# An attention and feed-forward block on one core: normalized rows turned by transposing DMAs, down products in their own PSUM bank, context parts split in one run

## The chip, the cores and the metric

The kernel runs on one core of a Trainium2 chip. The metric is the device time of one execution in microseconds, lower being better. The core has five engines with a queue each: PE (TensorE, matmuls), DVE (VectorE), ACT (ScalarE), POOL (GpSimd) and SP (SyncE, which here only issues DMAs). Engines wait for one another by semaphores alone.

## The reference

```python
h = tok_attention(x)                                   # 64 sequences, channels x 512 positions
h = h + attn(layernorm(h), Wq, Wk, Wv, Wo, qn_w, kn_w) # 16 heads, 4 kv heads, rms norm, rope, causal softmax
h = h + ffn(layernorm(h), w1, w2, w3)                  # bitlinear(sigmoid(x1) * x2), w quantized to -1, 0, 1
# ffn: x1 = y @ quant(w1).T ; x2 = y @ quant(w2).T ; out = (sigmoid(x1) * x2) @ quant(w3).T
```

The output has 64 x 32 rows of 512 numbers. The model width is 512, the head width 128, the feed-forward width 1408.

## The kernel before, in words

There are two stages. The first (`token_attention`) computes the token attention, writes its rows to `h1` in DRAM, and meanwhile converts the weights: the attention weights to pairs of float16 (a high and a low part), the feed-forward weights to ternary float16. The change does not touch it. The second (`blocks`) works through the 2048 rows in 16 tiles of 128 rows. Each engine has its own program, written out by hand in `body(n, attn, ffn)` and run over n = 0 to 16 by `over_tiles` (L654): n = 0 does attention alone, n = 1 to 14 is a loop, n = 15 and 16 are the last ones. Pass n works on the attention half of tile n and on the feed-forward half of tile n-1, interleaved.

The layernorm of a tile is computed with rows on partitions. The matmuls need it with features on partitions, in two float16 parts. In the kernel before PE does the turning: `transpose_x` (L1002) and `transpose_x2` (L1007) each issue four 128x128 float32 transposes into a PSUM bank (TR[0] and TR[1]); ACT copies the bank to the high part (`take_x` L729, L769), and DVE subtracts to get the low part (`x_low` L820, L890).

PE's order in a pass (L1098) is: projections c = 1 to 3 (`project`, 12 matmuls each, three products for each pair of parts), the transposes of x2n of tile n-1, projections 4 and 5; the gate products (`gate_products`, L1026 and L1027) of tile n-1 in six groups, with the transposes of rotated k and q (`transpose_qk`, L967 through `transpose`) and the scores (L1044) between them; the first 8 of 11 pairs of down products (L1062, L1063); the transposes of xn of tile n+1; the probabilities times the values (`weigh_values`, L1076); the other 3 pairs of down products; the projection c = 0 (keys) of tile n+1; and 48 output products (L1090 to L1092). Down products and output products accumulate in the same bank, PROJ[1], so the output products wait until DVE has read the down products (L942, semaphore `o_out`).

DVE makes the rotation of each projection (`rotate`, L832 to L847), the softmax chain (L910 to L930), the low context parts (`context_lo`, L867, four for each tile, behind ACT's four high parts L791), the result (L942) and the residual with its layernorm statistics (L953 and `ln_stats`). The result stands between the second and the third context part. POOL adds and scales the rotated projections (`rope_sum`, L700 to L707) and takes inverse square roots (L696). ACT squares, applies tanh and exp, and copies PSUM to SBUF.

Of the kernel before, what the change touches and what calls it, by code (L numbers as in the profile page):

```python
# [16 lines left out]
P = 128  # L17
# [551 lines left out]
def blocks(nc, W, h1, tables_in, norm_in, mask_in, ident_in, out):  # L569

    with ExitStack() as ctx:
# [9 lines left out]
        SCORES = TR[1]  # L581
# [14 lines left out]
        xh, xl = sb("x_hi", [P, D], F16), sb("x_lo", [P, D], F16)  # L596
# [20 lines left out]
        x2h, x2l = sb("x2_hi", [P, D], F16), sb("x2_lo", [P, D], F16)  # L617
# [9 lines left out]
        xt, x_hi, x_lo = sem("b_xt"), sem("b_x_hi"), sem("b_x_lo")  # L627
# [11 lines left out]
        xt2, x2_hi, x2_lo = sem("b_xt2"), sem("b_x2_hi"), sem("b_x2_lo")  # L639
# [10 lines left out]
        BANK = (PROJ[0], FB[2], FB[3], PROJ[0], PROJ[1], TR[0])  # L650
        DOWN_FIRST = 8
# [19 lines left out]
        @block.sync  # L671
        def _(sp):
            sp.dma_start(h_ln[:, :], h1[0:P, :]).then_inc(ln_in, DMA)
            for dst, src in ((tables[:, :, :], tables_in), (norm_w[:, :, :], norm_in), (mask[:, :], mask_in),
                             (ident[:, :], ident_in)):
                sp.dma_start(dst, src).then_inc(const_in, DMA)

            def body(n, attn, ffn):
                if attn and not (isinstance(n, int) and n + 1 >= NTT):
# [5 lines left out]
                if ffn:  # L685
                    sp.wait_ge(o_out, n + START)
                    sp.dma_start(out[bass.ds((n - 1) * P, P), :], o_tile[:, :]).then_inc(out_done, DMA)

            over_tiles(sp, body)
            sp.wait_ge(out_done, DMA * NTT + START)  # L690

        @block.gpsimd
        def _(pool):
# [14 lines left out]

            pool.wait_ge(const_set, 1)
            inv_std(0, 0, ln1_var, ln1_rstd)  # L710
            rope_sum(0, 0)
# [14 lines left out]
        def _(act):  # L726
            def take_x(n):
                act.wait_ge(xt, n + 1)
                nc.scalar.copy(xh[:, :], TR[0][:, :]).then_inc(x_hi, 1)  # L729
# [32 lines left out]
            def body(n, attn, ffn):  # L762
                last = isinstance(n, int) and n + 1 >= NTT
                if attn:
                    for c in range(1, KV):
                        square(n, c)
                if ffn:
                    act.wait_ge(xt2, n)
                    nc.scalar.copy(x2h[:, :], TR[1][:, :]).then_inc(x2_hi, 1)  # L769
                if attn:  # L770
                    square(n, KV)
                    act.wait_ge(proj, NPROJ * (n + 1))
                    nc.scalar.mul(v[:, :], BANK[NPROJ - 1][:, :], V_SHIFT).then_inc(v_out, 1)
                for f in range(NF):
                    for m in range(2):
# [5 lines left out]
                        if attn and (f, m) == (NF - 1, 1):  # L781
                            act.wait_ge(sub, n + 1)
                            nc.scalar.activation(pr[:, :, :], sd[:, :, :], ACT.Exp).then_inc(exped, 1)
                        if ffn and m == 1:
                            hidden_hi(n - 1, f)
                if attn:
                    if not last:
                        take_x(n + 1)
# [9 lines left out]
        def _(dve):  # L798
# [18 lines left out]

            def x_low(n):
                dve.wait_ge(x_hi, n + 1)
                nc.vector.tensor_tensor(xl[:, :], TR[0][:, :], xh[:, :], ALU.subtract).then_inc(x_lo, 1)  # L820
# [55 lines left out]
            x_low(0)  # L876
            rotate(0, 0)

            def body(n, attn, ffn):
# [5 lines left out]
                if attn:  # L885
                    for c in range(2, KV):
                        rotate(n, c)
                if ffn:
                    dve.wait_ge(x2_hi, n)
                    nc.vector.tensor_tensor(x2l[:, :], TR[1][:, :], x2h[:, :], ALU.subtract).then_inc(x2_lo, 1)  # L890
                if attn:
                    rotate(n, KV)
# [20 lines left out]
                if attn:  # L913
# [5 lines left out]
                    if not last:  # L919
                        ln_apply(n + 1, 0, h_ln[:, :], xn[:, :], ln1_rstd, ln1)  # L920
# [13 lines left out]
                if attn:  # L934
                    if not last:
                        x_low(n + 1)
                    for b in range(2):
                        context_lo(n, b)
                if ffn:
                    dve.wait_ge(w3, n)  # L940
                    dve.wait_ge(out_done, DMA * (n - 1) + START)
                    nc.vector.scalar_tensor_tensor(o_tile[:, :], PROJ[1][:, :], 2.0 ** -6, h2[:, :], ALU.mult, ALU.add  # L942
                                                   ).then_inc(o_out, 1)
                if attn:
                    for b in range(2, BT):
                        context_lo(n, b)
# [14 lines left out]
        def _(pe):  # L961
# [16 lines left out]
            def project(n, c):  # L978

                if c == 0:  # L980
                    pe.wait_ge(x_hi, n + 1)
                    pe.wait_ge(x_lo, n + 1)
# [9 lines left out]
                if c == 4 and not first:  # L992
                    pe.wait_ge(h2_done, n)
                pairs = []
                for k in range(KD):
                    at = (K_AT + k * KV * HD if c == 0 else V_AT + k * KV * HD if c == NPROJ - 1
                          else Q_AT + k * HEADS * HD + (c - 1) * D)
                    pairs.append((xh[:, k * P:(k + 1) * P], xl[:, k * P:(k + 1) * P],
                                  W.hi(at, D), W.lo(at, D)))
                split_products(BANK[c][:, :], pairs, proj)  # L1000

            def transpose_x(n):  # L1002
                pe.wait_ge(ln1, n + 1)
                pe.wait_ge(qkt_out, 5 * n)
                transpose(TR[0], xn, xt)

            def transpose_x2(n):  # L1007
                pe.wait_ge(ln2, n + 1)
                pe.wait_ge(taken, n + 1)
                transpose(TR[1], x2n, xt2)  # L1010

            def gate_products(n, f, m):

                if f == 0 and m == 0:
                    pe.wait_ge(x2_hi, n + 1)
                    pe.wait_ge(x2_lo, n + 1)
# [4 lines left out]
                for j, t in enumerate(FG[f]):  # L1021
                    for k in range(KD):
# [3 lines left out]
                        nc.tensor.matmul(dst, w, x2h[:, k * P:(k + 1) * P], start=(k == 0), stop=False)  # L1026
                        ins = nc.tensor.matmul(dst, w, x2l[:, k * P:(k + 1) * P], start=False, stop=(k == KD - 1))  # L1027
                ins.then_inc(f1, 1)

            def transpose_qk(n, c, ffn):  # L1030
                pe.wait_ge(q_ready, 5 * n + c + 1)
                if c == 0:
                    pe.wait_ge(v_out, n + 1)
                if c == 1 and ffn:
                    pe.wait_ge(x2_lo, n)
# [13 lines left out]
            def down_products(n, tiles):  # L1049
                if tiles[0] == 0:  # L1050
                    if isinstance(n, int) and n + 1 >= NTT:
                        pe.wait_ge(h2_done, n + 1)
                    else:
                        pe.wait_ge(squared, 5 * (n + 1) + 5)
                        pe.wait_ge(roped_b, 5 * (n + 1) + 5)
                for k in tiles:
# [5 lines left out]
                    nc.tensor.matmul(PROJ[1][:, :], hh[:, k, :], ffn_w[:, at:at + D], start=(k == 0), stop=False)  # L1062
                    ins = nc.tensor.matmul(PROJ[1][:, :], hl[:, k, :], ffn_w[:, at:at + D], start=False,  # L1063
# [16 lines left out]
            def output_products(n, ffn):  # L1080
                if ffn:
                    pe.wait_ge(o_out, n + START)
# [12 lines left out]
            transpose_x(0)  # L1095
            project(0, 0)

            def body(n, attn, ffn):  # L1098
                last = isinstance(n, int) and n + 1 >= NTT
                if attn:  # L1100
                    for c in range(1, NPROJ - 2):
                        project(n, c)
                if ffn:
                    transpose_x2(n - 1)
                if attn:
                    for c in range(NPROJ - 2, NPROJ):
# [13 lines left out]
                if attn and not last:  # L1120
                    transpose_x(n + 1)
# [4 lines left out]
                if attn:  # L1126
                    if not last:
                        project(n + 1, 0)
                    output_products(n, ffn)
# [61 lines left out]
```

## Time and profile before

| | |
|---|---|
| median of 3 runs | 1173.87 us (1173.56 to 1178.07) |
| profiled execution | 1172.51 us, of it span 1170.6 us |
| PE busy | 1093.5 us, 93% |
| DVE busy | 721.0 us, 62% |
| POOL busy | 433.5 us, 37% |
| ACT busy | 422.2 us, 36% |
| PE in the chain that ended last | 51% |

The first stage and the conversion of the weights end at about 390 us; the block stage takes the rest of the span. A page of the profile gives the busy time of each engine; the timeline lists each instruction with its start and duration, and in square brackets how long the engine had been idle before it and who released it. Matmuls are pipelined: the duration of one in the timeline is longer than the distance from its start to the next one's, and it is the distance that counts.

### The profile page before, as it was taken

What the parts mean: (1) busy time and instruction counts of PE and PEld (TensorE: products, weight loads), DVE (VectorE), ACT (ScalarE), POOL (GpSimd) and SP (SyncE); (2) the same over time, 40 slices, a digit from 0 to 9 for tenths busy, and PEclk for the clock granted to TensorE, in tenths of its full rate; (3) what the DMA queues carried; (4) which work ended last, traced back from release to release, by engine and by line L of the source; (5) the groups of instructions that cost most, each with busy time, mean ns of one, the idle gap of its engine ahead of it and who ended that gap; (6) DMA issues with size and microseconds to landing.
All of it is one profiled execution on the core that took longest, in us unless ns stands there. A gap on an engine that the chain in (4) does not pass through costs nothing.

```text
span 1170.6 us, 22169 instructions
## 1 busy us (share of the span) xinstructions
PE 1093.5 (93%) x8768; PEld 607.9 (52%) x8768; DVE 721.0 (62%) x1293; ACT 422.2 (36%) x733; POOL 433.5 (37%) x334
## 2 busy tenths in 40 slices
PE   4999989899989669999999999999999999999987
PEld 2434333433343235574664665756646657566465
DVE  6687766766685355566556655765666467556642
ACT  1666556455546122232332322313323224123231
POOL 2001027655555246144242361442433514514320
PEclk9999989989989779999999999999999999999999
DMA  6988835643541100000000000000000000000000
GB/s 182 305 312 272 292 116 150 179 132 116 158 133 50 57 10 10 18 9 27 18 9 27 18 9 27 0 27 18 9 27 18 9 27 0 27 18 9 18 11 10
DMA packets 35767, 83.81 MB, mean 72 GB/s; under 512 B 4496, under 2 KB 5264, under 8 KB 35728
## 3 DMA queue, kind: packets, MB, share of 16 engines
q1 hardware_dynamic: 35728, 83.26, 23.0%
q8 instruction: 27, 0.44, 0.2%
q14 instruction: 12, 0.10, 0.0%
HBM read 49.43 MB, written 8.39 MB: 49 GB/s over the span
## 4 chain that ended last, share of the span: by engine, by line
PE 51%; DVE 8%; issue 4%; POOL 2%; ACT 0%; DMA 0%; SPq 0%; DVEq 0%; POOLq 0%
PE ffn_sum L1026 5%; PE ffn_sum L1027 5%; PE proj L1090 5%; PE proj L1091 4%; PE proj L1092 4%; PE proj L973 3%; PE transposed L967 3%; PE proj L974 3%; PE proj L975 3%; PE ffn_sum L975 2%; PE ffn_sum L974 2%; PE ffn_sum L973 2%; PE ffn_sum L1076 2%; PE transposed L1044 1%; PE proj L1062 1%
## 5 line engine op out<-in xcount | busy, mean ns | idle before, releaser
L334 DVE TENSOR_REDUCE row_max<-score_rows 128x1 f32<-128x512 f32 x256 | 167.5, 686 | 90.5 <-PE score_rows L474 89.1
L700 POOL TENSOR_TENSOR roped<-rope_cos,rope_sin 128x512 f32<-128x512 f32 x80 | 101.7, 1271 | 324.8 <-DVE rope_sin L836 324.8
L293 ACT ACTIVATE exps<-score_cols 128x512 f32<-128x512 f32 x256 | 146.3, 600 | 136.4 <-PE score_cols L499 134.4
L1026 PE MATMUL ffn_sum<-x_hi,ffn_w 128*128 128x128 f16 x1408 | 166.9, 220 | 1.4 <-ACT x_hi L769 1.4
L1027 PE MATMUL ffn_sum<-x_lo,ffn_w 128*128 128x128 f16 x1408 | 166.8, 220 | 0.0
L474 PE MATMUL score_rows<-k_parts,q_parts 96*128 96x512 f32 x256 | 127.1, 510 | 16.4 <-DMA k_parts<-qk_low 15.1
L1026 PEld LDWEIGHTS ffn_sum<-x_hi,ffn_w 128*128 128x128 f16 x1408 | 138.1, 98 | 6.4 <-DVE hidden L853 3.0
L1027 PEld LDWEIGHTS ffn_sum<-x_lo,ffn_w 128*128 128x128 f16 x1408 | 138.4, 98 | 2.3
L474 PEld LDWEIGHTS score_rows<-k_parts,q_parts 96*128 96x128 f32 x256 | 53.4, 210 | 131.9 <-DVE row_max L334 73.7
L499 PE MATMUL score_cols<-q_parts,k_parts 98*128 98x512 f32 x256 | 110.0, 435 | 6.7 <-DMA q_parts<-max_t 4.4
L1090 PE MATMUL proj<-attn_slots,ctx_hi 128*128 128x512 f16 x256 | 97.0, 379 | 2.6 <-DVE ctx_lo L867 2.6
L735 ACT ACTIVATE squares<-ffn_sum 128x512 f32<-128x512 f32 x32 | 19.1, 597 | 220.2 <-PE ffn_sum L975 190.4
L1092 PE MATMUL proj<-attn_slots,ctx_lo 128*128 128x512 f16 x256 | 97.0, 379 | 0.0
L1091 PE MATMUL proj<-attn_slots,ctx_hi 128*128 128x512 f16 x256 | 97.0, 379 | 0.0
L248 POOL TENSOR_TENSOR qk_low<-qk_raw,qk_high 128x1024 fp32r<-128x1024 f32 x16 | 38.9, 2433 | 143.7 <-ACT qk_high L287 143.7
L707 POOL TENSOR_TENSOR roped<-roped,rms_inv 128x512 f32<-128x512 f32 x80 | 83.3, 1041 | 11.5
L703 POOL TENSOR_TENSOR rms_inv<-mean_sq,minus_half 128x4 f32<-128x4 f32 x80 | 85.2, 1066 | 3.3
L853 DVE SCALAR_TENSOR_TENSOR hidden<-tanh,ffn_sum 128x512 f32<-128x512 f32 (+1 forms) x48 | 30.8, 641 | 85.8 <-PE ffn_sum L1027 85.8
L953 DVE SCALAR_TENSOR_TENSOR h<-proj,o_unscale,h_res 128x512 f32<-128x512 f32 x16 | 12.0, 751 | 115.9 <-PE proj L1092 115.9
L973 PE MATMUL proj<-attn_slots,x_hi 128*128 128x512 f16 x192 | 74.4, 388 | 1.6 <-DVE x_lo L820 1.6
L974 PE MATMUL proj<-attn_slots,x_hi 128*128 128x512 f16 x192 | 74.3, 387 | 0.0
L975 PE MATMUL proj<-attn_slots,x_lo 128*128 128x512 f16 x192 | 74.2, 386 | 0.0
(124 smaller groups left out, 2010.9 us busy)
## 6 DMA issues: line engine op xcount, KB each, us to landing
raw_ffn<-in_w_ffn SPq DMA_DIRECT2D x24, 704.0 KB, 7.6
attn_slots<-in_w_attn SPq DMA_DIRECT2D x20, 512.0 KB, 11.3
qk_raw<-in_qk SPq DMA_DIRECT2D x16, 512.0 KB, 5.8
q_parts<-qk_high SPq DMA_DIRECT2D x32, 256.0 KB, 3.3
k_parts<-qk_high SPq DMA_DIRECT2D x32, 256.0 KB, 4.2
v_t<-in_v_t SPq DMA_DIRECT2D x16, 256.0 KB, 5.8
q_parts<-qk_low SPq DMA_DIRECT2D x16, 256.0 KB, 4.9
k_parts<-qk_low SPq DMA_DIRECT2D x16, 256.0 KB, 5.2
```

The costliest lines, as they stand in the source:

```text
L293: nc.scalar.activation(E[:, (STEPS * g + u) % NE, :], ST[(STEPS * g + u) % 3][:, :], ACT.Exp, scale=TOK_SCALE).then_inc(exp_done, 1)
L334: nc.vector.reduce_max(row_max[:, g % 2, k:k + 1], S[n % NS][:, :], AX.X).then_inc(s_free, 1)
L474: nc.tensor.matmul(bank[:, :], QP[g % NB][0:3 * CH, b, t * P:(t + 1) * P], KP[g % NB][0:3 * CH, b, :], start=True, stop=True).then_inc(s_f ...
L499: nc.tensor.matmul(ST[n % 3][:, :], KP[g % NB][0:3 * CH + 2, b, i * P:(i + 1) * P], QP[g % NB][0:3 * CH + 2, b, :], start=True, stop=True) ...
L973: nc.tensor.matmul(dst, ah, bh, start=(i == 0), stop=False)
L974: nc.tensor.matmul(dst, ah, bl, start=False, stop=False)
L975: t = nc.tensor.matmul(dst, al, bh, start=False, stop=(i == len(pairs) - 1))
L1026: nc.tensor.matmul(dst, w, x2h[:, k * P:(k + 1) * P], start=(k == 0), stop=False)
L1027: ins = nc.tensor.matmul(dst, w, x2l[:, k * P:(k + 1) * P], start=False, stop=(k == KD - 1))
L1090: nc.tensor.matmul(PROJ[1][:, :], ah, bh, start=(k == 0), stop=False)
L1091: nc.tensor.matmul(PROJ[1][:, :], ah, bl, start=False, stop=False)
L1092: ins = nc.tensor.matmul(PROJ[1][:, :], al, bh, start=False, stop=(k == HEADS - 1))
```

## The change

- The normalized rows are split before they are turned: ACT casts `xn` to `xhr` (float16, rows on partitions), POOL subtracts to get `xlr` for the first layernorm; for the second ACT makes `x2hr` and DVE `x2lr`. SP then issues one transposing DMA for each (`turn_x`, `turn_x2`), SBUF to SBUF, 128x512 float16, into `xh`, `xl`, `x2h`, `x2l` of shape 128 x 4 x 128. PE waits for 32 counts of `x_turned` or `x2_turned` for each tile. SP's program is written out for all 17 passes in place of the loop.
- PE has no transposes of x and x2 any more. The projection c = 0 of tile n+1 stands ahead of `weigh_values`, and the down products are divided into 4 pairs before and 7 pairs behind it.
- The down products accumulate in TR[0] (`DOWN`), the values' projection in TR[1].
- DVE splits all four context parts and then makes the result. The apply step of the next tile's layernorm moves ahead of the second `gate`, and ACT's cast of it behind the last copy of q.

```diff
-        SCORES = TR[1]
+        SCORES, DOWN = TR[1], TR[0]
-        BANK = (PROJ[0], FB[2], FB[3], PROJ[0], PROJ[1], TR[0])
-        DOWN_FIRST = 8
+        BANK = (PROJ[0], FB[2], FB[3], PROJ[0], PROJ[1], TR[1])
+        DOWN_FIRST = 4
@@ SP
+            def turn_x(n):
+                sp.wait_ge(x_hi, n + 1)
+                sp.dma_start(xh[:, :, :], xhr[:, :], transpose=True).then_inc(x_turned, DMA)
+                sp.wait_ge(x_lo, n + 1)
+                sp.dma_start(xl[:, :, :], xlr[:, :], transpose=True).then_inc(x_turned, DMA)
+            turn_x(0)
             def body(n, attn, ffn):
...
                 if ffn:
+                    turn_x2(n - 1)
+                if more:
+                    turn_x(n + 1)
+                if ffn:
                     sp.wait_ge(o_out, n + START)
                     sp.dma_start(out[bass.ds((n - 1) * P, P), :], o_tile[:, :]).then_inc(out_done, DMA)
@@ POOL
+            def x_low(n):
+                pool.wait_ge(x_hi, n + 1)
+                nc.gpsimd.tensor_tensor(xlr[:, :], xn[:, :], xhr[:, :], ALU.subtract).then_inc(x_lo, 1)
...
                     inv_std(n + 1, 0, ln1_var, ln1_rstd)
+                    x_low(n + 1)
                     rope_sum(n + 1, 0)
@@ ACT
             def take_x(n):
-                act.wait_ge(xt, n + 1)
-                nc.scalar.copy(xh[:, :], TR[0][:, :]).then_inc(x_hi, 1)
+                act.wait_ge(ln1, n + 1)
+                nc.scalar.copy(xhr[:, :], xn[:, :]).then_inc(x_hi, 1)
...
                 if attn:
-                    for c in range(1, KV):
+                    square(n, 1)
+                if ffn:
+                    act.wait_ge(ln2, n)
+                    nc.scalar.copy(x2hr[:, :], x2n[:, :]).then_inc(x2_hi, 1)
+                if attn:
+                    for c in range(2, KV + 1):
                         square(n, c)
...
+                        if attn and not last and (f, m) == (1, 0):
+                            take_x(n + 1)
@@ DVE
                     ln_apply(n - 1, 1, h2[:, :], x2n[:, :], ln2_rstd, ln2)
-                if attn:
-                    for c in range(2, KV):
+                if ffn:
+                    dve.wait_ge(x2_hi, n)
+                    nc.vector.tensor_tensor(x2lr[:, :], x2n[:, :], x2hr[:, :], ALU.subtract).then_inc(x2_lo, 1)
+                if attn:
+                    for c in range(2, KV + 1):
                         rotate(n, c)
...
                     hidden_lo(n - 1, 0)
+                if attn and not last:
+                    ln_apply(n + 1, 0, h_ln[:, :], xn[:, :], ln1_rstd, ln1)
+                if ffn:
                     gate(n - 1, 1)
...
-                    if not last:
-                        ln_apply(n + 1, 0, h_ln[:, :], xn[:, :], ln1_rstd, ln1)
...
                 if attn:
-                    if not last:
-                        x_low(n + 1)
-                    for b in range(2):
+                    for b in range(BT):
                         context_lo(n, b)
...
-                    for b in range(2, BT):
-                        context_lo(n, b)
@@ PE
                 if c == 0:
-                    pe.wait_ge(x_hi, n + 1)
-                    pe.wait_ge(x_lo, n + 1)
+                    pe.wait_ge(x_turned, 2 * DMA * (n + 1))
...
                 if tiles[0] == 0:
                     if isinstance(n, int) and n + 1 >= NTT:
-                        pe.wait_ge(h2_done, n + 1)
+                        pe.wait_ge(o_out, n + START)
                     else:
-                        pe.wait_ge(squared, 5 * (n + 1) + 5)
-                        pe.wait_ge(roped_b, 5 * (n + 1) + 5)
+                        pe.wait_ge(qkt_out, 5 * (n + 1) + 5)
...
                 if ffn:
                     down_products(n - 1, range(0, DOWN_FIRST))
                 if attn and not last:
-                    transpose_x(n + 1)
+                    project(n + 1, 0)
                 if attn:
                     weigh_values(n, ffn)
                 if ffn:
                     down_products(n - 1, range(DOWN_FIRST, KF))
                 if attn:
-                    if not last:
-                        project(n + 1, 0)
-                    output_products(n, ffn)
+                    output_products(n)
```

## Rows read from the trace of the kernel before

**Rows 1.** Windows, passes 1 to 14: us; busy (count) PE, PEld, DVE, ACT, POOL; clock, DMA.

```profile
448.84:1099.39 650.55, 644.37 (x5742) 399.13 (x5741) 396.58 (x770) 184.99 (x336) 247.89 (x238) 1.00 0.05 17
```

**Rows 2.** Waits of PE from 440 to 1170 us: total, times, longest.

```profile
PE ffn_sum L1076 <- DVE probs_t L930: 6.2, 14, 0.4
```

**Rows 3.** Timeline of PE, 707 to 741: start, duration, line, operation, operands, [idle before].

```profile
707.72 0.38 PE L1062 MATMUL proj<-ffn_w,hidden_hi 128*128 128x512 f16 x1
...
712.22 0.61 PE L1076 MATMUL ffn_sum<-probs_t,v 32*128 32x128 f32 x12 [0.44 <-DVE probs_t L930]
...
717.30 0.38 PE L1090 MATMUL proj<-attn_slots,ctx_hi 128*128 128x512 f16 x1
...
735.42 0.60 PE L967 MATMUL transposed<-ident,x2n 128*128 128x128 f32 x4
735.86 0.38 PE L973 MATMUL proj<-attn_slots,x_hi 128*128 128x512 f16 x1
...
741.04 0.22 PE L1026 MATMUL ffn_sum<-x_hi,ffn_w 128*128 128x128 f16 x1
```

**Rows 4.** Timeline of DVE in the same pass, 707 to 716.

```profile
707.94 0.69 DVE L917 TENSOR_TENSOR scores_less_max<-scores,row_maxima 128x512 f32<-128x512 f32 x1
...
714.07 1.29 DVE L867 TENSOR_TENSOR ctx_lo<-ffn_sum,ctx_hi 128x512 f16<-128x512 f32 x2 [0.88 <-ACT ctx_hi L791]
715.28 0.68 DVE L942 SCALAR_TENSOR_TENSOR out_tile<-proj,h 128x512 f32<-128x512 f32 x1
```

**Rows 5.** Timeline of DVE and PE in tile 0 and in pass 15.

```profile
435.16 2.48 DVE L867 TENSOR_TENSOR ctx_lo<-ffn_sum,ctx_hi 128x512 f16<-128x512 f32 x4 [2.33 <-ACT ctx_hi L791]
...
1126.14 0.69 DVE L917 TENSOR_TENSOR scores_less_max<-scores,row_maxima 128x512 f32<-128x512 f32 x1
...
1130.14 0.61 PE L1076 MATMUL ffn_sum<-probs_t,v 32*128 32x128 f32 x12 [0.60 <-issue]
```

**Rows 6.** Timeline of DVE, POOL, ACT and PE, 733 to 749.

```profile
733.80 0.53 DVE L815 TENSOR_SCALAR x2n<-h,mv,rstd 128x512 f32<-128x512 f32 x1
...
735.19 0.41 DVE L836 TENSOR_TENSOR rope_sin<-ffn_sum,tables 128x256 f32<-128x256 f32 x1
...
736.36 1.27 POOL L700 TENSOR_TENSOR roped<-rope_cos,rope_sin 128x512 f32<-128x512 f32 x1
...
745.55 1.04 POOL L707 TENSOR_TENSOR roped<-roped,rms_inv 128x512 f32<-128x512 f32 x1
...
747.10 0.64 ACT L747 ACTIVATE hidden_hi<-hidden 128x512 f16<-128x512 f32 x1
...
748.16 0.61 PE L967 MATMUL transposed<-ident,roped 128*128 128x128 f32 x4
...
748.86 0.58 ACT L756 COPY q_t<-transposed 128x512 f32<-128x512 f32 x1
```

**Rows 7.** DMA issues by line: count, KB each, median us to landing; first stage last.

```profile
out<-out_tile SPq DMA_DIRECT2D x16, 256.0 KB, 2.0
...
h_ln<-h_rows SPq DMA_DIRECT2D x13, 256.0 KB, 2.7
...
v_t<-in_v_t SPq DMA_DIRECT2D x13, 256.0 KB, 5.8
```

**Rows 8.** Timeline of DVE and PE at the stage's start and end.

```profile
395.06 0.55 DVE L815 TENSOR_SCALAR xn<-h_ln,mv,rstd 128x512 f32<-128x512 f32 x1
...
398.36 0.58 PE L973 MATMUL proj<-attn_slots,x_hi 128*128 128x512 f16 x1 [1.57 <-DVE x_lo L820]
...
422.82 0.66 PE L967 MATMUL transposed<-ident,roped 128*128 128x128 f32 x4 [2.73 <-POOL roped L707]
...
438.48 0.38 PE L1090 MATMUL proj<-attn_slots,ctx_hi 128*128 128x512 f16 x1
...
1148.52 0.55 DVE L815 TENSOR_SCALAR x2n<-h,mv,rstd 128x512 f32<-128x512 f32 x1 [0.67 <-POOL rstd L696]
...
1151.22 0.26 PE L1026 MATMUL ffn_sum<-x_hi,ffn_w 128*128 128x128 f16 x1 [1.45 <-ACT x_hi L769]
```

More of the change, by code:

```diff
@@ L595, in blocks @@
         xn = sb("xn", [P, D])
-        xh, xl = sb("x_hi", [P, D], F16), sb("x_lo", [P, D], F16)
+        xhr, xlr = sb("x_hi_rows", [P, D], F16), sb("x_lo_rows", [P, D], F16)
+        xh, xl = sb("x_hi", [P, KD, P], F16), sb("x_lo", [P, KD, P], F16)
         sq = [sb(f"squares{n}", [P, D]) for n in range(2)]
@@ L626, in blocks @@
         ln2_var, ln2_rstd, ln2 = sem("b_ln2_var"), sem("b_ln2_rstd"), sem("b_ln2")
-        xt, x_hi, x_lo = sem("b_xt"), sem("b_x_hi"), sem("b_x_lo")
+        x_turned, x_hi, x_lo = sem("b_x_turned"), sem("b_x_hi"), sem("b_x_lo")
         proj, squared, ssum, roped_a, roped_b = (sem("b_proj"), sem("b_squared"), sem("b_ssum"), sem("b_roped_a"),
@@ L676, in _, with turn_x2 @@
                 sp.dma_start(dst, src).then_inc(const_in, DMA)
+            def turn_x(n):
[3 more added lines that the diff above has]
+                sp.dma_start(xl[:, :, :], xlr[:, :], transpose=True).then_inc(x_turned, DMA)
+            def turn_x2(n):
+                sp.wait_ge(x2_hi, n + 1)
+                sp.dma_start(x2h[:, :, :], x2hr[:, :], transpose=True).then_inc(x2_turned, DMA)
+                sp.wait_ge(x2_lo, n + 1)
+                sp.dma_start(x2l[:, :, :], x2lr[:, :], transpose=True).then_inc(x2_turned, DMA)
+            turn_x(0)
             def body(n, attn, ffn):
-                if attn and not (isinstance(n, int) and n + 1 >= NTT):
+                more = attn and not (isinstance(n, int) and n + 1 >= NTT)
+                if more:
                     sp.wait_ge(ln1, n + 1)
@@ L685, in body @@
                 if ffn:
+                    turn_x2(n - 1)
+                if more:
+                    turn_x(n + 1)
+                if ffn:
                     sp.wait_ge(o_out, n + START)
                     sp.dma_start(out[bass.ds((n - 1) * P, P), :], o_tile[:, :]).then_inc(out_done, DMA)
-            over_tiles(sp, body)
+            for n in range(NTT + 1):
+                body(n, n < NTT, n > 0)
             sp.wait_ge(out_done, DMA * NTT + START)
@@ L993, in project @@
                     pe.wait_ge(h2_done, n)
+                if c == NPROJ - 1 and not first:
+                    pe.wait_ge(taken, n)
                 pairs = []
@@ L997, in project @@
                           else Q_AT + k * HEADS * HD + (c - 1) * D)
-                    pairs.append((xh[:, k * P:(k + 1) * P], xl[:, k * P:(k + 1) * P],
-                                  W.hi(at, D), W.lo(at, D)))
+                    pairs.append((xh[:, k, :], xl[:, k, :], W.hi(at, D), W.lo(at, D)))
                 split_products(BANK[c][:, :], pairs, proj)
[L1002 to L1010, printed above, removed]
             def gate_products(n, f, m):
                 if f == 0 and m == 0:
-                    pe.wait_ge(x2_hi, n + 1)
-                    pe.wait_ge(x2_lo, n + 1)
+                    pe.wait_ge(x2_turned, 2 * DMA * (n + 1))
                     pe.wait_ge(c_hi, KV * (n + 1))
@@ L1100, in body @@
                 if attn:
[L1101 to L1106, printed above, removed]
+                    for c in range(1, NPROJ):
                         project(n, c)
```

44 lines of the change are left out of this document (16 added, 28 removed).

## The prediction

> **What bounds the kernel now.** I read four views, in this order. First the windows: the fourteen loop passes that carry the whole change (n = 1 to 14) take 650.55 us, 46.47 us each, with PE busy 644.37 us and the granted clock at 1.00, that is the 2.4 GHz level [rows 1]. PE is the bound there, at full speed, so only what leaves PE's queue, or an idle gap of PE, can shorten a pass. Second the waits of PE: over the stage one gap repeats, 14 times 0.44 us, the product with the probabilities (L1076) waiting for the transposed probabilities from DVE [rows 2]. Third the timeline of PE in the pass that starts at 672 us. 24 projection matmuls stand between 735.86 and 741.04, so one costs 0.216 us; the transposes of x2n occupy PE from 735.42 to 735.86; behind the first down products, which begin at 707.72, and the transposes of xn, L1076 begins only at 712.22 [rows 3]. Fourth DVE and ACT beside it, to see what each wait of the new order would find [rows 4 to 6].
>
> **The change, part by part, in one pass (clock times are those of the pass in the rows).**
>
> *Transposes of x2n leave PE:* 0.44 us (735.42 to 735.86), nothing else was waited for there. Gain 0.44.
>
> *Transposes of xn leave PE, and the project(n+1, 0) block comes before the probability product.* Before, from the first down product (707.72) to L1076 (712.22) are 4.50 us, with 16 down products, the transposes and the gap. After, the same stretch holds 8 down and 12 projection matmuls: 20 x 0.216 = 4.32. Does DVE let L1076 start then? From the subtraction of the row maxima (707.94) to L1076 were 4.28 us. The apply step of xn sat in that stretch of DVE's program (L920), and it now moves ahead of the chain. In the last attention pass, which has no xn step, the same distance is 1126.14 to 1130.14, 4.00 us [rows 4, 5]. PE arrives 707.72 + 4.32 - 707.94 = 4.10 after the subtraction, so the softmax chain (4.00) is just hidden by 0.1 and the 0.44 us gap goes. Gain 4.50 - 4.32 = 0.18.
>
> *From L1076 to the output products.* Before 5.08 us (712.22 to 717.30) [rows 3]: the product, 6 down, 12 projection. DVE split two context parts (714.07), made the result (715.28), and split two more. After, PE holds the product (1.10) and 14 down products (3.02), 4.12; but the output products want all four parts, and these now run without the result between. In tile 0, where nothing was between, four took 2.48 us [rows 4, 5]: 714.07 + 2.48 + 0.15 of release = 716.70, which is 4.48 after L1076's start. So this part is bound by ACT and DVE, with a new stall of 0.36 us on PE. Gain 5.08 - 4.48 = 0.60. Bounds: 0.96 if the parts come in time, 0.00 if ctx_lo still needs what it needed before.
>
> *The result (L942)* waits for the last down product, now at about the time the fourth part ends; it comes 1 us later than before and pushes rotate(n+1, 0) by as much. POOL, its reader, has nothing else between the fifth q part of one pass and that rotation, and DVE then waits for the 48 output products (10.35 us, 48 x 0.216). Transposes of q and k in TR[0] wait for the result, half a pass later. All at nothing. The down products have their own bank, so the output products no longer wait for the result: it was already out of the way, nothing. The result's store and the next h_ln load are issued behind it on SP, 1 us later, while h_ln is not read before the rotations of the next pass: nothing.
>
> *x2 turned by DMAs.* x2n ends at 734.33 (733.80 + 0.53). ACT's cast from SBUF takes 0.64, DVE's subtraction 0.69, as its other steps of this shape [rows 4, 6]: high rows at 735.0, low rows at 735.75. The gate products, first readers, start at 741.04 - 0.44 = 740.60. So the second DMA may take up to **4.85 us** from issue to landing. Behind these waits on SP stand the next x's DMAs and the result's store, which come later anyway. DVE waits for ACT here, and rotate(n, 2) starts 1.44 us later; POOL, busy with the part before, took that part up only at 736.36 where it was ready at 735.60, so the q parts come some 0.7 later. The fifth was ready at 745.55 + 1.04 = 746.59 and its transposes on PE began at 748.16 [rows 6]; with 747.3 against 747.72, 0.4 remains. Cost nothing, 0.4 us of cover; were POOL another us late, a pass would cost 0.6 more.
>
> *x turned by DMAs.* ACT casts x behind the last q copy: 748.86 + 0.58 - 0.44 = 749.0, plus 0.64. The new POOL subtraction is not in the trace; nearest is POOL's addition of the same shape, 1.27 [rows 6] (bounds: 1.04, the multiplication's row, to 2.5, twice the row). Low rows at 751.0. project(n+1, 0) comes at 754.19 (707.72 + 46.47) - 0.44 + 8 x 0.216 = 755.47. So this DMA may take up to **4.4 us**. ACT, while it waits for xn, holds the next hidden_hi, which stands behind two more groups of gate products: nothing.
>
> *What a transposing DMA takes.* No row shows one. Nearest are the plain DMAs of this stage: 256 KB from SBUF in 2.0 us, to SBUF in 2.7 (ours have half the bytes). In the heavy traffic of the first stage a load of 256 KB lands in 5.8 [rows 7]. DMA share here is 0.05 [rows 1]. I take 3.0 for the second of a pair (2.7 and a little for the one ahead of it), with 2.0 and 5.8 as ends. At 3.0 both are hidden.
>
> The Trainium skill speaks on both sides. "VectorE: DVE Perf Modes", The three transpose paths, gives 1309 ns for a 128x128 block by DMA (390 ns by TensorE) and says to use TensorE if a PSUM destination is acceptable. If that price held per block, an estimate from the page is 4 x 1.3 = 5.2 us for each transfer and 10.5 for a pair; the second would land some 9.8 us after its issue, and by my slope below the kernel would be about 155 us slower. "Advanced Engine Details and Errata", X-Bar Transpose, says that transposing DMAs are as fast as regular ones, which would be my 2.0 to 2.7. No row of before decides between them.
>
> *Sum of a pass:* 0.44 + 0.18 + 0.60 = 1.22 us; x 14 = **17.1 us**.
>
> *Edges.* Start: xn ended at 395.61 and the first projection began at 398.36, 2.75 later; after: cast 0.64, POOL 1.27, DMA 3.0, some 5.2: **+2.4**. Tile 0: its last q transposes began at 422.82; in a pass x's low rows come 3.3 after these (751.0 + 0.44 - 748.16), here at 426.1, landed 429.1; twelve projections take 2.6 at the full clock and 5.2 at half, I take 3.9 behind the idle time, 433.0; and 4.48 on is 437.5 against 438.48: **-1.0**. Pass 15: 0.44 + 0.60 = **-1.0**. Last gate products: x2n ends 1149.07, they began 1151.22; after: 0.64 + 0.69 + 3.0 + releases = 1153.4: **+2.2** [rows 5, 8]. Together +2.6.
>
> Net -14.5: span 1170.6 becomes 1156.1, with the 1.9 us around the span 1158.0. That execution (1172.51) was 1.36 below the median of the runs, 1173.87, so **1159.4 us**.
>
> **The rivals.** With t for the second DMA's time from issue to landing, beyond 4.85 each us costs 28 in the passes (two stalls in each of 14) and 4 at the edges, 32 in all; at 4.9 the gain is gone.
> (A) *The turned rows land late*: PE waits before the gate products and before project(n+1, 0). At t = 5.8 (the row of v_t) a pass changes by -1.22 + 0.95 + 1.40 = +1.13, x 14 = 15.8, and the edges by +12 (2.6 and 3 x 2.8, and 1.0 in pass 15): about **1202 us**. For it: nothing measured is a transposing DMA, two are on one queue, PE is full around both. Against: the stage's DMA rows are 2.0 to 2.7 and the cover is 4.4.
> (B) *The context chain keeps PE where it was*: if ACT's casts and DVE's parts need the 5.08 us of before, or POOL's extra work delays the q parts, a pass gains 0.44 + 0.18 only, 8.7 us in all, 2.6 given back: **1168 us**. For it: the end of a pass is bound by this chain in my own sum. Against: tile 0's four parts.
> (C) *PE idles less than the rows say, or the DMAs take 4.6 to 5.1*: gain and stalls cancel, about **1174 us**.
>
> **How the numbers follow.** Forecast 0.50, (A) 0.30, (B) 0.13, (C) 0.07. A difference of 0.5% (5.9 us) is about what a measurement of this kernel can tell from no change. Of (B) half lies within it: faster 0.50 + 0.06, same 0.07 + 0.07, slower 0.30. Lower end: no context stall (-5) and t = 2.0 (-3): 1152. Upper end: (A) at t = 5.8, 1202; beyond lies some 0.17. The forecast's own range is 1152 to 1166.
>
> **What would show it.** Right: passes of about 45.25 us; no PE transposes of x; the transposing DMAs landing below 4.4 us; no PE wait before L1026 and L973; a small one (0.3 to 0.4) before L1090 on ctx_lo; none or under 0.1 before L1076. Wrong: PE waits released by DMA x_hi or x_lo fourteen times (A); waits of L1090 near 1 us or of L967 on POOL's roped (B). A transposing DMA that holds SP's queue for microseconds would also break the sum, since the low rows queue behind the high ones.

## The result and the profile after

The changed kernel takes **1163.37 us** (median of 6 runs, 1161.4 to 1164.11) against 1173.98 us for the kernel before in the same comparison: a ratio of **0.9908, 95% interval 0.9894 to 0.9921**. That is 0.9% faster. I had forecast 1159.4 us, 1.2% faster, in a range of 1152 to 1202 (1152 to 1166 for the forecast's own case). The profiled execution took 1163.83 us, with a span of 1161.7 us, 8.9 less than that of before.

The head of the page of the changed kernel:

```profile
span 1161.7 us, 21798 instructions
## 1 busy us (share of the span) xinstructions
PE 1078.6 (93%) x8640; PEld 592.2 (51%) x8640; DVE 721.7 (62%) x1277; ACT 419.9 (36%) x733; POOL 463.8 (40%) x350
```

PE has lost 15 us of work (1093.5 before). POOL has gained 30 us: 18.6 for its 16 new subtractions (1.16 each), 7.4 because its 32 inverse square roots (L718) take 0.78 us each where they took 0.55, and 3.0 in its multiplications (L729). Why the old steps take longer was not tried. The windows of the changed kernel run from the output products (L1096) of one pass to those of another: the first row is fourteen passes, the second the last thirteen of them. The columns are those of [rows 1].

```profile
440.44:1076.66 636.22, 633.61 (x5629) 385.85 (x5630) 397.73 (x756) 183.09 (x336) 275.29 (x252) 1.00 0.11 28
487.07:1076.66 589.59, 587.16 (x5227) 357.99 (x5228) 370.07 (x703) 170.01 (x312) 255.63 (x234) 1.00 0.11 29
```

Thirteen passes take 589.59 us, **45.35 us each where they took 46.47** [rows 1]. The fourteenth, which is the first, took 636.22 - 589.59 = 46.63; more on it below. By PE's busy time a pass lost 0.86 us of work (644.37 / 14 = 46.03, now 587.16 / 13 = 45.17), which is twice the 0.44 us of four transposes, and 0.25 us of idle time (0.44 before, 0.19 now).

The waits of PE from 390 us on (small ones left out): total, times, longest:

```profile
PE proj L991 <- DMA x_lo<-x_lo_rows: 15.9, 2, 13.6
PE ffn_sum L1033 <- DMA x_lo<-x_lo_rows: 7.7, 1, 7.7
PE proj L1096 <- DVE ctx_lo L891: 5.9, 15, 3.3
PE ffn_sum L1082 <- issue: 2.3, 1, 2.3
```

The gap before the probability product [rows 2] is gone. A small one before the output products has come, 0.19 us in a pass. A turning DMA is waited for in no pass from 1 to 15, only at the edges: before the first projection of all (13.6 us of idle time, of which the last 4.6 lie behind the end of xn), before the projection c = 0 of tile 1 in tile 0's pass (2.3) and before the last gate products (7.7). Here is one pass in the timeline of PE, the counterpart of [rows 3]:

```profile
737.14 0.22 PE L1033 MATMUL ffn_sum<-x_hi,ffn_w 128*128 128x128 f16 x1
...
744.26 0.28 PE L985 MATMUL transposed<-ident,roped 128*128 128x128 f32 x1
...
750.29 0.38 PE L1068 MATMUL transposed<-ffn_w,hidden_hi 128*128 128x512 f16 x1
...
752.01 0.38 PE L991 MATMUL proj<-attn_slots,x_hi 128*128 128x512 f16 x1
...
754.70 0.39 PE L1082 MATMUL ffn_sum<-probs_t,v 32*128 32x128 f32 x4
...
759.18 0.38 PE L1096 MATMUL proj<-attn_slots,ctx_hi 128*128 128x512 f16 x1 [0.19 <-DVE ctx_lo L891]
```

From the first down product to the probability product are 4.41 us (4.50 before), and from there to the output products 4.48 (5.08 before). The projections lose the 0.44 us of x2n's transposes. 0.44 + 0.09 + 0.60 = 1.13, the 1.12 us of a pass. These three are lengths of stretches, and the third is shorter mostly because the 12 projections left it for the second and 8 down products came the other way.

The queue of SP and the engines that feed it, in the same pass. The DMAs that turn x2 come first, those that turn x second:

```profile
731.55 0.69 DVE L910 TENSOR_TENSOR x_lo_rows<-x2n,x_hi_rows 128x512 f16<-128x512 f32 x1 [0.68 <-ACT x_hi_rows L796]
...
731.54 1.20 SPq L688 DMA_TRANSPOSE x_hi<-x_hi_rows  x1
732.79 1.26 SPq L690 DMA_TRANSPOSE x_lo<-x_lo_rows  x1
...
742.88 1.04 POOL L729 TENSOR_TENSOR roped<-roped,rms_inv 128x512 f32<-128x512 f32 x1
...
746.46 1.16 POOL L733 TENSOR_TENSOR x_lo_rows<-xn,x_hi_rows 128x512 f16<-128x512 f32 x1 [1.49 <-ACT x_hi_rows L757]
...
746.41 1.19 SPq L682 DMA_TRANSPOSE x_hi<-x_hi_rows  x1
747.65 1.26 SPq L684 DMA_TRANSPOSE x_lo<-x_lo_rows  x1
```

And the issues of these DMAs (30 of the 32 pairs), with the median us from issue to landing:

```profile
x_hi<-x_hi_rows SPq DMA_TRANSPOSE x30, 2.4
x_lo<-x_lo_rows SPq DMA_TRANSPOSE x30, 2.5
```

The last transfers are issued at 732.79 and 747.65, 4.35 and 4.36 us before PE reads what they bring (737.14 and 752.01), and land after 2.5. So 1.8 to 1.9 us of cover are left, if this reading is right.

### The profile page after: what moved, and what is told of

Its sections match the earlier page's. It is cut to its first block, busy times and chain, and to the rows that moved or that the text cites. A ratio compares the mean times of both kernels' runs of the same rounds, so it can differ in the third digit from the quotient of the medians.

```text
span 1161.7 us, 21798 instructions
## 1 busy us (share of the span) xinstructions
PE 1078.6 (93%) x8640; PEld 592.2 (51%) x8640; DVE 721.7 (62%) x1277; ACT 419.9 (36%) x733; POOL 463.8 (40%) x350
## 4 chain that ended last, share of the span: by engine, by line
PE 55%; issue 4%; DVE 3%; POOL 2%; ACT 1%; DMA 1%; SPq 0%; POOLq 0%; DVEq 0%
PE ffn_sum L1033 7%; PE ffn_sum L1034 6%; PE proj L1096 5%; PE proj L1098 4%; PE proj L1097 4%; PE proj L991 3%; PE proj L993 3%; PE proj L992 3%; PE transposed L985 3%; DVE ctx_lo L891 2%; PE ffn_sum L993 2%; PE ffn_sum L991 2%; PE ffn_sum L992 2%; PE ffn_sum L1082 2%; PE transposed L1069 1%
## 5 line engine op out<-in xcount | busy, mean ns | idle before, releaser
L499 PE MATMUL score_cols<-q_parts,k_parts 98*128 98x512 f32 x256 | 108.6, 430 | 10.5 <-DMA q_parts<-max_t 6.2
L1096 PE MATMUL proj<-attn_slots,ctx_hi 128*128 128x512 f16 x256 | 97.5, 381 | 5.9 <-DVE ctx_lo L891 5.9
L729 POOL TENSOR_TENSOR roped<-roped,rms_inv 128x512 f32<-128x512 f32 x80 | 86.3, 1078 | 11.5
L718 POOL TENSOR_TENSOR rstd<-var,minus_half 128x1 f32<-128x1 f32 x32 | 25.0, 782 | 148.8 <-DVE var L838 148.8
```

The costliest lines, as they stand in the source:

```text
L499: nc.tensor.matmul(ST[n % 3][:, :], KP[g % NB][0:3 * CH + 2, b, i * P:(i + 1) * P], QP[g % NB][0:3 * CH + 2, b, :], start=True, stop=True) ...
L1096: nc.tensor.matmul(PROJ[1][:, :], ah, bh, start=(k == 0), stop=False)
```

## The experiments

Twelve more runs were made, two of them repeats of a kernel. Theory: a pass is shorter by what left PE's queue and by a shorter way through the context parts, and the DMAs are hidden with 1.8 us to spare. Rivals: the new order and the bank alone bring the gain; or the landings already decide when PE goes on. To compare passes I use the same window for each kernel, thirteen passes from the output products of pass 1 to those of pass 14; one execution is enough for that, since the middle passes of a kernel agree closely (where single ones differ, it is said).

**Both turned by PE again.** PE's order, the banks and the undivided context parts stay; ACT's and DVE's steps on x and x2 read PSUM again and stand about where they stood before. This is the core of the edit:

```diff
+            def transpose_x2(n):
+                pe.wait_ge(ln2, n + 1)
+                pe.wait_ge(o_out, n + START)
+                pe.wait_ge(qkt_out, 5 * n + 5)
+                transpose(TR[0], x2n, xt2)
+            def transpose_x(n):
+                pe.wait_ge(ln1, n + 1)
+                if not (isinstance(n, int) and n == 0):
+                    pe.wait_ge(taken, n)
+                transpose(TR[1], xn, xt)
...
+                if attn and not last:
+                    transpose_x(n + 1)
                 if ffn:
                     down_products(n - 1, range(0, DOWN_FIRST))
```

> The new order, banks and splits stay, but both x and x2 are turned by PE again (x2 through TR[0], x through TR[1], before the first down products). Theory (the gain of a pass is what left PE's queue, and only the DMAs can take it away): two sets of transposes come back, 2 x 0.44, a pass of 46.2 us in place of 45.35; the start and the last gate products get 1.9 and 3.2 us back; about 1171 us in all, not told from the kernel before. Rival (the reordering, the bank of the down products and the undivided context parts bring the gain, the DMAs only move work): a pass of 45.4 or less, about 1160 us.

Measured: 1173.44 us, ratio to the kernel before 0.9991 (0.9972 to 1.0009). The window:

```profile
486.19:1089.12 602.93, 600.49 (x5330) 368.77 (x5331) 368.07 (x716) 167.69 (x312) 229.79 (x221) 1.00 0.05 17
```

602.93 / 13 = 46.38 us. Of the 1.12 us gained in a pass, 1.03 go with the DMAs; the order, the bank and the context parts without them keep 0.09. The rival of the order alone falls. What the down products' own bank is worth by itself was not tried: every new kernel has it. What the order is worth beside the context parts shows further down, where the place of the result is undone.

**Only x2 turned by PE** (the part of the edit above on x2).

> Only x2 is turned by PE again, x by DMAs as in the changed kernel. Theory: pass 45.35 + 0.44 = 45.79 us, and the end 3.2 us shorter, because the last gate products no longer wait for a DMA: about 1166 us. Rival (ordering alone): pass stays 45.35.

```profile
485.36:1080.65 595.29, 592.84 (x5279) 364.01 (x5279) 361.48 (x703) 168.15 (x312) 244.88 (x234) 1.00 0.08 23
```

595.29 / 13 = 45.79 us, the expected value to the hundredth; 1165.16 us in one execution. x's part is then 46.38 - 45.79 = 0.59: four transposes (0.44) and 0.15 that PE spends between the last of the first down products and the projection. There the projection has x_lo to wait for, which ACT and DVE make inside the softmax stretch; but x_lo ended 0.35 us before the projection began, so that this wait is the 0.15 is not shown.

**One and two more transposing DMAs ahead of each pair**, into spare tiles, with PE waiting for all:

```diff
                 sp.wait_ge(x_hi, n + 1)
+                for s in spare:
+                    sp.dma_start(s[:, :, :], xhr[:, :], transpose=True).then_inc(x_turned, DMA)
                 sp.dma_start(xh[:, :, :], xhr[:, :], transpose=True).then_inc(x_turned, DMA)
...
-                    pe.wait_ge(x_turned, 2 * DMA * (n + 1))
+                    pe.wait_ge(x_turned, 3 * DMA * (n + 1))
```

> One more transposing DMA (into a spare tile) ahead of each pair; PE waits for all three. It puts some 1.25 us on both landings. Theory (the DMAs have 1.8 us of cover in a pass): pass stays 45.35 us, only start, tile 0 and end grow, 1.25 us each, about 1167 us. Rival (the landing already decides): 2 x 1.25 more in each pass, 47.8 us, about 1200 us.

> Two more transposing DMAs ahead of each pair, 2.5 us on both landings. Theory (1.8 us of cover): the last 0.65 us show at both waits, a pass of 46.6 us, PE waiting for DMA x_lo before the gate products and before the projection c = 0; about 1188 us. Rival (landing already decides): a pass of 50.3 us. If the cover is larger than I read, the pass stays 45.35.

The windows with one and with two more:

```profile
491.01:1080.60 589.59, 587.15 (x5226) 357.88 (x5227) 370.19 (x703) 170.03 (x312) 255.58 (x234) 1.00 0.14 35
```

```profile
497.16:1105.79 608.63, 591.50 (x5227) 355.98 (x5227) 370.26 (x703) 168.78 (x312) 248.85 (x234) 1.00 0.16 39
```

With one more a pass is 45.35 us, unchanged to the hundredth, though both landings come 1.25 us later (1166.82 us in all). With two more it is 46.82, and PE waits where it should, between 500 and 1070 us:

```profile
PE ffn_sum L1039 <- DMA x_lo<-x_lo_rows: 7.9, 12, 0.9
PE proj L997 <- DMA x_lo<-x_lo_rows: 5.7, 12, 0.5
```

A pass grows by 1.47, that is 0.73 for each wait on average (the list gives 0.66 and 0.48, counted from the modelled end of the product before), where 2.5 - 1.8 = 0.7 was to come. So the cover is 1.8 us, and the landing decides nothing in the changed kernel. The execution took 1194.79 us, 7 more than expected; start and end wait for these DMAs uncovered.

**The place of the result undone**: two context parts, the result, two context parts.

```diff
-                    for b in range(BT):
+                    for b in range(2):
                         context_lo(n, b)
...
+                    for b in range(2, BT):
+                        context_lo(n, b)
                     if not last:
                         rotate(n + 1, 0)
```

> In the changed kernel only the order of DVE is undone: two context parts, the result, two context parts. Theory (with 14 down products behind the probability product the result ends last, and the third and fourth part wait for it): from L1082 to the output products 4.2 + 0.7 + 1.3 + 0.15 = 6.3 us in place of 4.48, a pass of 47.2 us, about 1189 us. Rival (the place of the result is indifferent, as it was in the kernel before): pass 45.35.

PE's waits of this kernel in the same stretch, DVE in one pass, and three windows: PE's output products in two passes, and one whole pass.

```profile
PE proj L1098 <- DVE ctx_lo L891: 26.0, 12, 2.2
```

```profile
676.84 0.69 DVE L962 SCALAR_TENSOR_TENSOR out_tile<-transposed,h 128x512 f32<-128x512 f32 x1 [1.29 <-PE transposed L1071]
677.45 1.28 DVE L891 TENSOR_TENSOR ctx_lo<-ffn_sum,ctx_hi 128x512 f16<-128x512 f32 x2
```

```profile
629.85:641.90 12.05, 12.05 (x49) 5.09 (x50) 2.45 (x5) 0.00 (x0) 3.33 (x3) 0.86 0.09 29
678.87:689.23 10.36, 10.36 (x49) 4.69 (x49) 2.45 (x5) 0.00 (x0) 3.33 (x3) 1.00 0.10 34
629.85:678.87 49.02, 46.85 (x402) 27.91 (x403) 28.47 (x55) 13.08 (x24) 19.66 (x18) 0.97 0.10 27
```

The result waits for the last down product, and the third and fourth context part wait for the result, as expected. The wait before the output products is 2.17 us, and a pass takes 47.33 us, 1.98 more than 45.35 (1.75 to 1.85 expected). The place of the result cost nothing in the kernel before, where PE had no wait at its output products in a pass; in the new order, with 14 down products behind the probability product, it is worth more than everything else. Beside that comes something not expected: in three of the fourteen passes the granted clock fell after that same wait (the 48 output products that begin at 629.85 take 12.05 us at 0.86, those at 678.87 take 10.36 at 1.00), and these passes took 48.9 to 49.0 us. In all 1197.32 us, in one execution, in place of 1189.

**The probability products sequence by sequence, and two sequences at a time**, so that ACT may begin earlier:

```diff
-                for h in range(KV):
-                    for b in range(BT):
+                for b in range(BT):
+                    for h in range(KV):
...
-                ins.then_inc(pv, 1)
+                    ins.then_inc(pv, 1)
...
-                    act.wait_ge(pv, n + 1)
                     for b in range(BT):
+                        act.wait_ge(pv, BT * n + b + 1)
```

> The probability products go sequence by sequence instead of head by head, and ACT may take each context part when its four products are done. Theory (the stretch from L1082 to the output products is bound by the chain product, ACT cast, four DVE parts, 4.48 us against 4.12 of PE): the chain starts some 0.8 us earlier, PE becomes the bound at 4.2 us, the wait on ctx_lo goes, a pass of 45.1 us, about 1159.5 us. Rival (the 0.19 us is a hand-over that comes with any wait): pass stays 45.35. Third possibility: products of one row group in sequence take longer, and the pass grows.

The timeline of PE around the product, sequence by sequence, then in the changed kernel, head by head:

```profile
717.26 2.82 PE L1082 MATMUL ffn_sum<-probs_t,v 32*128 32x128 f32 x32
720.01 0.39 PE L1068 MATMUL transposed<-ffn_w,hidden_hi 128*128 128x512 f16 x1
```

```profile
709.35 1.17 PE L1082 MATMUL ffn_sum<-probs_t,v 32*128 32x128 f32 x32
710.45 0.39 PE L1068 MATMUL transposed<-ffn_w,hidden_hi 128*128 128x512 f16 x1
```

Measured: 1185.85 us, ratio 1.0100 (1.0077 to 1.0123), a pass of 46.65. The third possibility holds: the same 32 records take 2.75 us (720.01 - 717.26) in place of 1.10. The wait on ctx_lo is indeed gone, but PE itself pays for it. Together with the edges (below) it made 1178.8 us, 1.0039 (1.0019 to 1.0059), where 1153.5 was expected, since this half of it costs instead of gaining:

> Both of the two preceding edits. If they add: about 1153.5 us, 1.75% below the kernel before. If the wait on ctx_lo wasn't the bound: 1157 us.

> The changed kernel with the probability products of sequences 0 and 1 first, then of 2 and 3, ACT taking parts as each half is done. In the version sequence by sequence the 32 products took 2.75 us, head by head 1.10. Theory (products on different 32-row groups overlap, those on the same one follow one another at 0.086 us each): two groups in turn take about half of 2.75, 1.4 us; ACT starts some 0.4 us earlier after their start than before; a pass of 45.4 to 45.5. Rival (any change of order costs the full 2.75): 46.65.

Two sequences at a time: 1162.11 us in one execution, a pass of 45.55, and the product takes 1.65 us. So the cost depends on how many sequences take turns: 0.086 us for each record with one, 0.052 with two, 0.034 with four. Each sequence has its own 32-row group of the array, and also its own PSUM bank (`FB[b]`), so these runs don't tell whether the row group or the bank makes the difference; the theory names the first. It is a near miss: the product is 0.55 longer, and the 14 down products behind it reach the output products in 3.03 us in place of 3.38, which gives back 0.35, the listed wait of 0.19 among it.

**The edges.** PE turns the first x and the last x2, where it is idle anyway, and pass 15, which has no projection of a next tile, has 8 pairs of down products first:

```diff
+            pe.wait_ge(ln1, 1)
+            transpose(TR[1], xn, xt)
             project(0, 0)
...
+                if ffn and not attn:
+                    pe.wait_ge(ln2, n)
+                    pe.wait_ge(taken, n)
+                    transpose(TR[1], x2n, xt2)
+                first_down = 8 if last and attn else DOWN_FIRST
```

> The changed kernel, with PE turning the first x and the last x2, and 8 pairs of down products ahead of the probability product in pass 15. Theory (my edges were mis-sized there): start -1.9, pass 15 -1.35 (4.48 in place of 5.83, since the clock doesn't fall in an idle time of 2.3 us), end -3.2 (2.3 of waiting, 0.9 of low clock): about 1157 us, passes unchanged at 45.35. Rival (the edges are a property of that run): 1163 us.

> The first x and the last x2 turned by PE and 8 pairs of down products first in pass 15, once more beside the changed kernel, since four executions spread from 1152.6 to 1163.4. Theory: start, pass 15 and end are 6 us shorter, so the median lies about 6 us below the changed kernel's, near 1157.5. Rival (the low clock after an idle time takes back in tile 0 and pass 1 what the edges give): within 3 us of the changed kernel.

> The changed kernel once more, as the yardstick on the same chip for the two beside it: passes of 45.35 us, about 1163.4 us.

First 1160.59 us over four executions (1152.59 to 1163.38), ratio 0.9895 (0.9873 to 0.9918); again 1158.29 over five (1156.57 to 1161.58), 0.9883 (0.9865 to 0.9901), beside 1162.51 and 0.9908 (0.9892 to 0.9925) of the changed kernel. The medians are 4.2 us apart in the second comparison, between the 6 of the theory and the 3 of its rival, and the intervals overlap. What the trace shows without doubt are the two waits. The last gate products, first of the changed kernel run again, then with this edit:

```profile
1140.33 0.29 PE L1033 MATMUL ffn_sum<-x_hi,ffn_w 128*128 128x128 f16 x1 [7.71 <-DMA x_lo<-x_lo_rows]
```

```profile
1135.07 0.27 PE L1050 MATMUL ffn_sum<-x_hi,ffn_w 128*128 128x128 f16 x1 [1.45 <-ACT x_hi L795]
```

From pass 15's first output product to here are 18.23 and 15.93 us: 2.30 saved. At the start, from xn's end to the first projection, 4.64 became 2.81: 1.83 saved. Together 4.1, close to the difference of the medians; as executions of one kernel lie up to 5 us apart (up to 11 in the first four), the closeness is partly luck. The rest of my 6 us, pass 15, did not come: in the changed kernel run again pass 15 took 45.23 us, as with the edit; the 46.50 of its first profile were a clock fall that this execution had and the other did not.

**Three pairs of down products first** in place of four, on top of the edges:

```diff
-        DOWN_FIRST = 4
+        DOWN_FIRST = 3
```

> As edges_again, with 3 pairs of down products ahead of the projection c = 0 and 8 behind the probability product. Theory (a pass is bound by two chains, softmax up to L1099 at 4.22 us after the first down product, and context parts 4.48 after it): the probability product starts at 4.22 in place of 4.41, PE arrives at the output products after 1.10 + 16 x 0.216 = 4.55, the wait on ctx_lo goes, a pass of 45.23 us, 1.7 us less than edges_again in all. If it stays at 45.35, 0.1 us of hand-over takes it back.

```profile
525.86 0.39 PE L1099 MATMUL ffn_sum<-probs_t,v 32*128 32x128 f32 x4 [0.31 <-DVE probs_t L962]
```

```profile
485.04:1075.10 590.06, 585.97 (x5228) 358.84 (x5227) 370.23 (x702) 170.16 (x312) 255.67 (x234) 1.00 0.11 29
```

1160.14 us, ratio 0.9904 (0.9888 to 0.992), a pass of 45.39. The wait on ctx_lo went, as expected, but one of 0.31 us for the softmax chain came. The probability product starts 4.37 us after the first down product, so this chain needs 4.37 and not 4.22, and in the changed kernel, where the product starts at 4.41, it is hidden by 0.04 us only. Of the two divisions tried in the new order, 4 to 7 is the better by 0.04 us a pass; in the medians the two can't be told apart (1158.29 and 1160.14).

## Why the prediction came out as it did

The direction, the mechanism and the place of each effect in a pass were right; at the edges the sizes were not. The gain was smaller than forecast, 10.6 us in the medians and 8.9 in the spans, against 14.5. Term by term, forecast and measured in the profiled span:

| | forecast | measured |
|---|---|---|
| start, to the first projection | +2.4 | +1.9 |
| tile 0, to its output products | -1.0 | +0.1 |
| fourteen passes | -17.1 | -14.3 |
| pass 15 | -1.0 | +0.2 |
| to the last gate products, and these | +2.2 | +3.2 |
| sum | -14.5 | -8.9 |

Of the 5.6 us that are missing, 2.8 are in the fourteen passes and 2.8 at the edges (+2.6 forecast, +5.4 measured).

- **x2's transposes**: 0.44 forecast, 0.44 measured, and shown by the kernel that gives them back to PE (45.79).
- **Up to the probability product**: 4.32 forecast, 4.41 measured. The term was 20 matmuls by 0.216, and it left out 0.1 us of hand-over before L1082, which the 0.44 us gap of before had hidden. Fourteen times this is 1.3 us of the missing 2.8. The softmax chain, which I had put at 0.1 us under PE, is at 0.04.
- **Up to the output products**: 4.48 forecast, 4.48 measured, taken from tile 0's four parts in one run. The stall of 0.36 is there too: 14 down products cover 3.38 us up to the next start, against 3.02 by 0.216 each; the list shows 0.19 of it, since it counts from the modelled end of the last product. This was the step in which the change could have failed, as its undoing shows (47.33).
- **What a transposing DMA takes**: 3.0 us from the low rows' being ready were taken, and it was 2.5 (x) and 3.05 (x2, whose low rows stand behind the high ones in SP's queue by 0.55). Each holds SP for 1.2 us, where a plain one of this stage holds it for 0.3 to 0.4, at most 0.6; I had only named that as a danger. The cover I counted from issue, 4.85 and 4.4, was 4.35 and 4.36: the first was too long by the queue, the second right.
- **POOL's extra 1.3 us and DVE's wait**: the fifth q part was ready at 743.92, and its transposes began at 744.26: 0.34 of cover, forecast 0.4. POOL's subtraction takes 1.16, forecast 1.27.
- **Rival (A), late landings**: not so. One more DMA in front costs nothing in a pass, two cost 1.47.
- **Rival (B), the context chain**: not so, but only because DVE's order was changed with it.
- **Rival (C), gain and stalls that cancel**: not so. The DMAs land 2.5 us after their issue, and no pass waits for one.
- **The edges were mis-sized**, by 2.8 us in all, half of what is missing, and mostly by the clock. In tile 0 the twelve projections were put at 3.9 us, between both levels; they took 5.23 at a granted clock of 0.50, the 1.2 GHz level (the kernel before took 4.06 for them at 0.63):

```profile
430.49:435.72 5.23, 5.23 (x13) 1.64 (x13) 2.97 (x5) 0.63 (x1) 0.00 (x0) 0.50 0.16 53
```

One part was overlooked: the changed kernel has idle times of PE in new places, 3.32 us in tile 0 before the output products (project(1, 0) stood there before) and 2.33 in pass 15 before the probability product. After these the clock can fall; it need not. In pass 15 the kernel before idled as well, 2.57 us before its output products, and these ran at 1.00:

```profile
1135.29 0.38 PE L1090 MATMUL proj<-attn_slots,ctx_hi 128*128 128x512 f16 x1 [2.57 <-DVE ctx_lo L867]
```

The output products of tile 0 in three executions, of the changed kernel, of the same one run again, and of the one with x2 by PE:

```profile
440.44:452.08 11.64, 11.64 (x49) 5.03 (x49) 2.44 (x5) 0.00 (x0) 3.33 (x3) 0.89 0.00 0
```

```profile
439.24:452.28 13.04, 13.04 (x48) 5.35 (x49) 2.45 (x5) 0.00 (x0) 3.34 (x3) 0.79 0.00 0
```

```profile
439.56:449.92 10.36, 10.36 (x49) 4.70 (x49) 2.45 (x5) 0.00 (x0) 3.33 (x3) 1.00 0.00 0
```

The same 48 products behind the same wait take 11.64, 13.04 and 10.36 us, at a granted clock of 0.89, 0.79 and 1.00. In the kernel before they take 10.36, with no wait ahead. So this loss is 0 to 2.7 us by the execution; it explains 1.3 us of the first pass and, in pass 15, the difference between 46.50 and 45.23. With 45.23 the term of pass 15 comes to -1.0 (46.26 before), as forecast, so that the term failed in one execution and held in the next is chance. From the last gate products to the end the changed kernel takes 0.9 us more. The clock's part was in no term of mine but the 3.9. That another order in tile 0 would avoid it was not tried.

The Trainium skill, in "VectorE: DVE Perf Modes", The three transpose paths, prices a 128x128 block (of bf16) at 1309 ns by DMA; my estimate from it was 10.5 us for a pair and a kernel 155 us slower. The pair landed 3.8 us after its first issue (731.54 to 732.79 + 2.5), and each further transfer of four blocks was issued, and landed, 1.25 us later. So the page's figure doesn't multiply with the blocks of one transfer: four took 2.4 to 2.5 us. What a single block takes no run here shows. The same page's rule (Rules for kernel authors), to use TensorE where a PSUM destination is acceptable, would have cost 1.03 us in every pass here, since PE was the bound and the queue of SP was free. The Trainium skill's "Advanced Engine Details and Errata", X-Bar Transpose, calls these transfers as fast as regular ones. The landing of one is near that of a plain one of twice the bytes (2.5 us for 128 KB, beside 2.0 to 2.7 for 256 KB, [rows 7]), which bears this out in part only, and the issuing queue does not: 1.2 us against 0.3 to 0.4.

## What to carry to other kernels

Where PE is the bound and works almost without gaps, as here, turning tiles by transposing DMAs gained little more than the time of the transposes that left PE (0.88 of 1.12 us), and only because the split into two float16 parts moved ahead of the turning and the landing was covered; measure the cover by putting a useless transfer in front. When a block is moved past others, ask what it had been hiding: here the projection had covered both the context parts and an idle time in tile 0, and the place of one DVE instruction (the result) decided between 1.1 us gained and 0.9 lost in a pass. At the ends of a kernel, where PE is idle, the way with the shorter latency is the better one: here PE's transposes were 4.1 us shorter there.

## What the runs showed of the hardware

- A transposing DMA of 128x512 float16 from SBUF to SBUF holds the issuing queue for 1.19 to 1.32 us and lands 2.4 to 2.5 us after its issue; further ones in the same queue are issued, and land, 1.25 us apart.
- Sixteen float32 products of 32 rows (32 records), each of the four 32-row groups writing its own PSUM bank: 1.10 us if the four take turns, 1.65 with two in turn and 2.75 if each has its four products in a row. Row group or bank was not separated.
- PE's clock can fall from the 2.4 to the 1.2 GHz level after an idle time of only 1.6 to 3.3 us, and does so in some executions and passes and not in others with the same wait: in three of fourteen equal passes behind 2.17 us, 1.6 to 1.7 us lost each time; behind 3.3 us in tile 0, in eight of ten traces, 1.3 to 2.9 us lost; behind 1.62 us in tile 0 in both traces of the product sequence by sequence.
